# Attention over pairs of key tiles: where the second product stands in TensorE's order

## The reference, cut to what matters

```
q_r    = einsum('bshq,hqr->bhsr', q_big, W_qr)
k_r    = einsum('bld,hdr->bhlr', kv_rope, W_kr)
scores = einsum('bhsr,bhlr->bhsl', q_r, k_r)
attn   = softmax(scores, axis=-1)
ctx_c  = einsum('bhsl,bld->bhsd', attn, kv_rope)
```

## Time and profile before

| | |
|---|---|
| median of three runs | 3513.51 us |
| span of the profiled execution | 3514.6 us, 38874 instructions |
| PE busy | 3164.6 us, 90% |
| DVE busy | 2422.4 us, 69% |
| POOL busy | 1775.2 us, 51% |
| ACT busy | 1444.3 us, 41% |
| PE, mix (L835) | 747.5 us in 3072 rows, idle before it 0.8 us |
| PE, scores (L820, L823) | 521.1 and 443.3 us |
| PE, scores for the maxima (L801) | 403.9 us |

### The profile page before, as it was taken

One profiled execution on the slowest core, in us unless ns is written; L12 is line 12 of the kernel. 1 busy time (PEld: TensorE's weight loads), 2 busy tenths in 40 slices (PEclk: granted clock), 3 DMA queues, 4 the chain that ended last, 5 costly groups with the idle time before them and its releaser, 6 DMA issues. The chain is left out here.

```text
span 3514.6 us, 38874 instructions
## 1 busy us (share of the span) xinstructions
PE 3164.6 (90%) x13320; PEld 1894.7 (54%) x13320; DVE 2422.4 (69%) x3194; ACT 1444.3 (41%) x2131; POOL 1775.2 (51%) x1048
## 2 busy tenths in 40 slices
PE   7699978999789997899988799789998899789997
PEld 6455556555465554655546555465545555455545
DVE  3578756787567885678865688557856687557865
ACT  3235533354332553425534445334542454334542
POOL 0467624676246762367632477226741476226740
PEclk9899989999899998999998899899998899899998
DMA  7400012000121000210002100110010100110010
GB/s 257 118 13 14 5 55 80 25 14 5 42 86 32 10 10 33 86 38 14 10 28 79 44 10 10 47 39 14 14 42 6 48 14 5 47 43 10 14 47 6
DMA packets 74831, 133.06 MB, mean 38 GB/s; under 512 B 7252, under 2 KB 49924, under 8 KB 73208
## 3 DMA queue, kind: packets, MB, share of 16 engines
q1 hardware_dynamic: 74616, 130.26, 11.7%
HBM read 116.96 MB, written 13.04 MB: 37 GB/s over the span
## 5 line engine op out<-in xcount | busy, mean ns | idle before, releaser
L1164 POOL TENSOR_TENSOR sum_pool<-sum_pool,prob 125x896 f32<-125x896 f32 x472 | 998.2, 2115 | 221.5 <-ACT prob L1051 217.1
L1051 ACT ACTIVATE prob<-wide 125x896 f32<-125x896 f32 x768 | 703.9, 917 | 888.7 <-PE wide L823 880.7
L1276 DVE TENSOR_REDUCE maxpart<-single 128x1 f32<-128x500 f32 x1344 | 824.0, 668 | 261.4 <-PE single L801 261.0
L835 PE MATMUL single<-prob,kv 125*64 125x448 f32 x3072 | 747.5, 565 | 0.8
L820 PE MATMUL wide<-qhigh,kparts 128*125 128x448 f32 x1536 | 521.1, 421 | 0.0
L820 PEld LDWEIGHTS wide<-qhigh,kparts 128*125 128x125 f32 x1536 | 231.2, 189 | 471.7 <-issue 469.6
L823 PE MATMUL wide<-qlow,kones 65*125 65x448 f32 x1536 | 443.3, 370 | 0.0
L801 PE MATMUL single<-kparts,qhigh 128*128 128x500 f32 x1344 | 403.9, 408 | 22.8 <-DVE kparts L1244 11.8
L823 PEld LDWEIGHTS wide<-qlow,kones 65*125 65x125 f32 x1536 | 291.3, 190 | 29.8
L801 PEld LDWEIGHTS single<-kparts,qhigh 128*128 128x128 f32 x1344 | 255.8, 191 | 84.2 <-issue 32.3
L1164 POOL TENSOR_TENSOR sum_pool<-prob 125x896 f32<-125x896 f32 x64 | 135.0, 2110 | 311.2 <-ACT prob L1051 311.2
(11 more groups left out here) (272 smaller groups left out, 4863.1 us busy)
## 6 DMA issues: line engine op xcount, KB each, us to landing
wexp_low_values<-in_experts SPq DMA_DIRECT2D x68, 384.0 KB, 3.1
raw<-in_ctx SPq DMA_DIRECT2D x66, 375.0 KB
w_low_values<-w_merged SPq DMA_DIRECT2D x64, 192.0 KB, 2.4
w_low_values<-wabs_merged SPq DMA_DIRECT2D x64, 128.0 KB, 2.3
w<-w_merged SPq DMA_DIRECT2D x64, 96.0 KB, 1.9
wo_raw<-in_wo SPq DMA_DIRECT2D x2, 2048.0 KB, 21.0
wq_raw<-in_wq SPq DMA_DIRECT2D x2, 2048.0 KB, 28.9
kcq_raw<-in_kcq SPq DMA_DIRECT2D x2, 1536.0 KB, 24.2
```

What stands on the lines that cost most here:

```text
L835: mm = pe.matmul(mix_acc[64 * half:64 * half + DC, 0:HQ], kv[:, j % 3, t, :], prob[:, (j * LT + t) % NPROB, half * HQ:(half + 1) * HQ], st ...
L1051: nc.scalar.activation(prob[:, n_ % NPROB, :].rearrange("p (a b) -> p a b", a=2), acc[0:LP, :, 0:HQ], ACT.Exp)\
L1164: nc.gpsimd.tensor_tensor(dst, first_in, prob[:, n_ % NPROB, :], ALU.add).then_inc(s["pool_sum"], 1)
L1276: V.tensor_reduce(maxpart[:, j % 2, t, b:b + 1], acc[:, 0:LB], AX.X, ALU.max).then_inc(*R.signal_drained(kind, *key))
```

## The change

The mixes are held back and issued in pairs. At odd t, after `score` and `smax` of that tile, the two mixes of the preceding pair are issued; at even t, none. `context` stays directly behind the mix of tile 11. The rest of the list is as it was. The number of instructions and their sizes stay the same.

```diff
-    last = None
+    waiting, fresh = [], []
...
-            if last is not None:
-                add("mix", *last)
-                if last[1] == LT - 1:
-                    add("context", last[0])
-            last = (j, t)
+            fresh.append((j, t))
+            if t % 2:
+                for tile in waiting:
+                    add("mix", *tile)
+                    if tile[1] == LT - 1:
+                        add("context", tile[0])
+                waiting, fresh = fresh, []
             if 0 < j < BG - 1 and t == 0:
                 keys(j + 1)
             if t == 1 and j:
...
-    add("mix", *last)
+    for tile in waiting:
+        add("mix", *tile)
     add("context", BG - 1)
```

## The result

The changed kernel takes 3703.41 us (median of four runs, 3700.11 to 3705.11), the kernel before 3512.66 in the runs beside it (3510.21 to 3513.51). The ratio is 1.0544, with a 95% interval from 1.0531 to 1.0557: 5.4% slower. Forecast were 3702 us. The profiled execution has a span of 3701.3 us and a mean granted clock of 0.917, against 3514.6 and 0.939.

A forecast was written before the change was run, and what follows sets the result against it. PE's own issue was taken to set the pace, with DVE nearly as busy. Batches with keys +192 us, the rest -34 and the clock +29 made +187 on 3514.6: 3702 us, range 3560 to 3775.

The forecast's parts named there:

- The saving: PE: 336 merged fp32 stretches save 0.34 us each, 114 us; with 11 at groups' ends, 125; a pair takes 1.67.
- merging saves nothing: Rival, 4%: edges of PE's fp32 stretches move inside the pair, so all the waits but no gain, 3816 us.
- `norm`: PE waits 3.8 us at `norm`, starting at T + 14.9, for DVE's adds, queued behind the key subtractions.
- the first rival: Rival, 20%: DVE's adds go one behind the other, wait 2.1 us shorter, clock stays at 1.00, 3572 us.
- The turn that the forecast took from the earlier trace: A POOL instruction coming during a DVE add goes ahead of the next add; POOL's sum here takes 2.10 us.
- The maxima's banks: Products for the maxima wait for DVE to empty banks: 1.2 us behind `norm`, 0.45 per pair, whose period is 5.33.
- a bracket on L804's matmuls: Sign in the new profile: the products for the maxima (L804) carry a bracket that names maxpart.
- The clock: PE at 0.50 for 3.41 us behind each `norm` wait: 0.6 us lost, 48 times, +29 us; bounds 0 and 1.7.
- The sum: 48 batches with keys +192 us, rest of the groups -34, clock +29: total +187, giving 3702 us; 66% chance.
- the bound of 1.7: Upper bound in us on PE work lost to the lower clock behind one `norm` wait.
- The rest of the run: Parts of each group outside its six batches with keys: 8 x -4.2 = -34 us.
- everything stays covered: Rival, 8%: DVE delivers both adds and the third bank in time, leaving the 125 us saved, 3389 us.

The follow-up runs named there:

- 7: Kernel before, single mixes, with the next batch's `keys` moved ahead of the mix of tile 11: 3789.64 us, ratio 1.0776.
- 9: Changed kernel plus 15 extra matmuls ahead of `norm`'s wait in 48 of 64 batches: 3662.94 us, ratio 1.0441.
- 4: Changed kernel with POOL's first sum of a batch held until DVE's two adds are done: 3600.2 us, ratio 1.0257.
- 1: Changed kernel with DVE's two adds put in a step of their own before `keys`: 3493.94 us, ratio 0.9949.
- 2: Changed kernel with the products for the maxima spread over the tiles, some behind the mixes: 3650.69 us, ratio 1.0399.
- 10: The kernel of 2 plus the same 15 extra matmuls ahead of `norm`'s wait as in 9: 3566.71 us, ratio 1.0155.
- 3: Changed kernel with the edits of 1 and 2 together, adds ahead of the keys and maxima spread: 3386.63 us, ratio 0.9646.

## Why the prediction was right

The steps can be held against the trace one by one. The table gives means over the 48 batches with keys, from the starts of PE's rows, in us: from `maxT` to `norm`, on to the next mix, and on to the next `maxT`. Without pairs the next mix comes behind one tile's scores and maxima, with pairs behind two, so the first two rows compare only with each other in these columns.

| kernel | to `norm` | to mix | to `maxT` | batch |
|---|---|---|---|---|
| before | 9.07 | 2.57 | 18.55 | 30.19 |
| 7, keys first, no pairs | 12.66 | 4.37 | 18.74 | 35.77 |
| changed | 12.32 | 6.11 | 16.48 | 34.92 |
| 9, filler | 12.28 | 5.32 | 16.49 | 34.09 |
| 4, POOL later | 10.57 | 5.60 | 16.49 | 32.66 |
| 1, adds first | 8.84 | 5.30 | 16.49 | 30.63 |
| 2, spread | 12.31 | 5.21 | 16.45 | 33.98 |
| 10, spread and filler | 12.28 | 3.42 | 16.45 | 32.14 |
| 3, adds first, spread | 8.75 | 3.40 | 16.44 | 28.59 |

**The saving.** Right. A pair takes 1.66 against the 1.67 forecast; exactly 336 late loads of the scores' weights are gone; and experiment 3, in which little is late, is 124.5 us faster than before, against 125. The rival "merging saves nothing" is out. Experiment 3 spreads the maxima too, and no run spreads them without pairs. What that alone would give is not measured; the place where the kernel before holds them up, 0.91 against 0.78 in the earlier trace rows, is worth 48 x 0.13, some 6 us.

**`norm`.** Right to 0.1 us. T + 14.90 was forecast, 14.90 is in the row; POOL goes between the adds; the wait is 3.68 against 3.8. Experiment 1 shows that the adds' place is the cause, 7 that it is enough by itself, and 4 that POOL's turn is 1.75 of it. In 4 the adds do run one behind the other, as the first rival had it; it takes 103 us off, where that rival's 2.1 us and full clock would have taken 130. The Trainium skill ("SBUF — State Buffer", "🔬 SBUF: two separate sides") has a DVE instruction with two SBUF inputs and a GpSimd instruction that reads SBUF contend for a common port pair, which goes to the one that starts first, for the whole instruction. The trace agrees: POOL's sum starts at 1225.14, the second add at 1225.85, and the add takes 2.84 instead of 1.09. The turn that the forecast took from the earlier trace rows needs one row more. In the kernel before, POOL's rope_s (1202.03 to 1203.89) came during the add below and went ahead of the add at 1203.05, which took 1.79:

```profile
1201.12 1.90 DVE L1297 TENSOR_TENSOR sum_dve<-prob 125x896 f32<-125x896 f32 x1
```

**The maxima's banks.** Right. From `norm` to the mix I had 5.30 with the clock left aside. Experiments 9 and 1, where the clock holds, show 5.32 and 5.30. A pair's period is 5.33 (1234.48 to 1239.81), as forecast. Spreading the maxima takes 1.9 of the 5.30 away. Some 0.7 of that is three products that now stand behind the mix (0.78 with an edge in the earlier trace rows), and the 1.2 left is the wait of the forecast. The prediction looked for this wait as a bracket on L804's matmuls. There only 4.8 us name the banks, as before; the wait shows on their weight loads.

**The clock: the term that was mis-sized.** The sum had 0.6 us for each of 48 waits, 29 us. Between the changed kernel and experiment 9 the stretch behind `norm` differs by 0.79 us and the time by 40.5 us. The mechanism was as described, the size 0.2 too small. Where DVE does not set the time, between experiments 2 and 10, the same drop costs 1.79 us a batch, more than the bound of 1.7, and 84 us in all. That also is the excess of experiment 2.

The granted clock in the traces shows what the term lacked. The sum took one stretch of 3.41 us at 0.50, as in the earlier trace rows. In the changed kernel 34 of the 48 batches have just that, and they take 5.81 us from `norm` to the mix, 0.49 more than in experiment 9. In the other 14 the clock stays at 0.50 for 6.83 us, from within the wait on, and from `norm` to the mix they take 6.83 as well, 1.51 more than in experiment 9. In experiment 2 it is again 34 and 14 batches, at 1.53 and 2.44 more than in experiment 10: the bound of 1.7 holds where the low stretch is a single one.

In 7, the stretch to the mix grew by 1.80, 86 us over 48 batches, and the 3.59 before it make 172: 258 of its 277 over the kernel before.

The Trainium skill ("TensorE: Matmul & The Clock Gate", "HAM oscillation — how this bites in real kernels") reckons the loss as half of the time spent at the lower clock. From the spans and mean clocks, the time at half speed is 2 x (1 - 0.915) x 3649.2 = 620 us in experiment 2 and 2 x (1 - 0.940) x 3563.9 = 428 in experiment 10. Half of the difference, an estimate by that rule, is 96 us, and 84 were measured. For the changed kernel and experiment 9 it is 614 and 410: by the rule 102, measured 40.5. The rule is near where PE sets the pace, and too high where another engine does.

**The sum.** 48 batches cost 4.73 us each more than before (34.92 against 30.19), 227 us; 4.60 were forecast, clock included. The rest of the run, the spans' 186.7 less 227, gives 40 back, 34 forecast. The two errors, 6 us each, cancel: that the total came within 2 us of the forecast is in part luck. (Against the runs beside it the change costs 190.8 us; 187 were forecast.) The time of "everything stays covered" (3389) is what the kernel reaches with the adds ahead of the keys and the maxima spread (3386.63).

## What to carry to other kernels

Where an instruction list is shared by all engines, moving one step moves its part on every engine: here a change made for PE's sake put DVE's adds behind the keys, and that cost 209 us, more than the 125 that it could save. With the adds ahead but the maxima not spread, their banks leave only 17 of the 125. A regrouping that saves edges on one engine is worth its gain only together with the reordering that keeps the others early: with the adds ahead and the maxima spread, the same pairs are 3.5% faster than the kernel before. And what one repair is worth depends on the other: spreading the maxima gives 107 us with the adds early (experiments 1 and 3), but 53 with the adds late (the changed kernel and 2). Most of the difference is the clock, since with the filler in both kernels it gives 96 (9 and 10).

## What was not expected of the hardware

- The clock fell to 0.50 behind waits of 1.93 us as well, in 31 of 48 batches, and not in the other 17 with the same wait (experiment 4). I had expected 1.00 in all.
- Work that the result does not need can pay: 15 extra matmuls in each of 48 waits kept the clock at 1.00 behind them and made the changed kernel 40.5 us faster and experiment 2 84 us faster.
- The price of a lower clock is not one number: 0.79 us a batch behind DVE's chain, 1.79 where PE sets the pace.
